# One table for all engines in the first chunk of a transformer block: x in two halves, weight groups between single products, three banks

## The reference

```
x = x + 0.5 * ffn(layernorm(x))
x = x + attention(layernorm(x))         # 16 heads of 16, causal
x = x + 0.5 * ffn(layernorm(x))
ffn:  W = LUT[4-bit codes] * scales     # gate, up: 2048 x 256; down: 256 x 2048; blocks of 32
      out = (gelu_tanh(x @ Wg.T) * (x @ Wu.T)) @ Wd.T
```

## Time and profile before

| what | us |
|---|---|
| median of 3 runs | 990.78 (986.47 to 992.03) |
| the profiled execution | 992.37 |
| its span, first to last instruction | 990.6 |
| TensorE busy | 926.6 |
| first product of the first chunk starts | 24.13 |
| first product of the second chunk starts | 107.91 |

### The profile page before, as it was taken

One profiled execution on the slowest core, in us unless ns is written; L12 is line 12 of the kernel. 1 busy time (PEld: TensorE's weight loads), 2 busy tenths in 40 slices (PEclk: granted clock), 3 DMA queues, 4 the chain that ended last, 5 costly groups with the idle time before them and its releaser, 6 DMA issues.

```text
span 990.6 us, 16766 instructions
## 1 busy us (share of the span) xinstructions
PE 926.6 (94%) x6726; PEld 408.9 (41%) x6726; DVE 611.1 (62%) x994; ACT 479.2 (48%) x650; POOL 230.5 (23%) x261
## 2 busy tenths in 40 slices
PE   2899999999989999888999989999999998999998
PEld 2456544554534545223544322244442222445444
DVE  6984345756777687677778767768785550242221
ACT  2454242033165330787332389963319999742240
POOL 3663573035002430000432000005200000052240
PEclk9999999999999999899999999999999999999999
DMA  7000050014000060000060000000000000000000
GB/s 262 1 1 1 1 96 11 2 57 52 2 2 2 25 83 2 1 1 2 1 107 2 22 2 2 1 1 1 2 22 2 1 2 2 2 1 1 22 1 21
DMA packets 19755, 20.26 MB, mean 20 GB/s; under 512 B 3040, under 2 KB 18400, under 8 KB 19680
## 3 DMA queue, kind: packets, MB, share of 16 engines
q1 hardware_dynamic: 16192, 15.93, 8.3%
q10 hardware_dynamic: 3488, 3.28, 1.0%
HBM read 12.78 MB, written 6.29 MB: 19 GB/s over the span
## 4 chain that ended last, share of the span: by engine, by line
PE 78%; ACT 6%; DVE 6%; issue 6%; DMA 2%; POOL 1%; SPq 0%; ACTq 0%; DVEq 0%; POOLq 0%
PE ps L1124 12%; PE ps L1095 12%; PE ps L1096 11%; PE ps L1097 11%; PE ps L1274 9%; PE ps L1229 7%; ACT inter L742 6%; PE ps L1125 6%; PE ps L1257 4%; DVE sg L1035 2%; DVE sg L1032 1%; PE ps L1241 1%; PE ps L1200 1%; PE ps L1080 1%; DMA xres<-in_L_attn_x 1%
## 5 line engine op out<-in xcount | busy, mean ns | idle before, releaser
L742 ACT ACTIVATE inter<-ps 128x1024 f32<-128x1024 f32 (+3 forms) x320 | 265.9, 898 | 34.9 <-PE ps L1241 19.3
L637 POOL TENSOR_TENSOR inter<-wreg,inter 128x512 f16<-128x512 f32 x112 | 129.3, 1158 | 644.6 <-ACT inter L723 644.4
L1035 DVE TENSOR_REDUCE sg<-ps 128x2 f32<-128x1024 f32 (+3 forms) x217 | 220.2, 1037 | 49.2 <-PE ps L1241 24.4
L752 ACT ACTIVATE wreg<-ps,gelu_in 128x512 f32<-128x512 f32 x112 | 77.1, 688 | 269.9 <-PE ps L1097 269.8
L1124 PE MATMUL ps<-wd,inter 128*128 128x512 f16 x512 | 170.8, 380 | 0.0
L1032 DVE TENSOR_REDUCE sg<-ps 128x1 f32<-128x512 f32 (+3 forms) x206 | 120.8, 632 | 64.7 <-PE ps L1229 43.7
L901 DVE SCALAR_TENSOR_TENSOR wreg<-ps,kappa,wreg 128x512 f32<-128x512 f32 x128 | 95.6, 748 | 102.8 <-PE ps L1097 97.0
L1274 PE MATMUL ps<-inter,v 128*17 128x512 f32 (+3 forms) x1280 | 150.1, 541 | 0.7
L1125 PE MATMUL ps<-wd,inter 128*128 128x256 f16 x512 | 139.5, 273 | 0.0
L1229 PE MATMUL ps<-kreg,qreg 48*128 48x512 f16 (+3 forms) x640 | 109.6, 355 | 18.4 <-DVE sg L1035 11.6
L1257 PE MATMUL ps<-qreg,kreg 50*128 50x512 f16 (+3 forms) x640 | 110.2, 354 | 16.2 <-ACT inter L742 10.6
(11 more groups left out here) (130 smaller groups left out, 890.6 us busy)
## 6 DMA issues: line engine op xcount, KB each, us to landing
qk_split<-oT SPq DMA_DIRECT2D x4, 1024.0 KB, 4.5
kreg<-qk_split SPq DMA_DIRECT2D x24, 128.0 KB, 4.7
qreg<-qk_split SPq DMA_DIRECT2D x24, 128.0 KB, 8.2
xres<-in_L_attn_x ACTq DMA_DIRECT2D x4, 512.0 KB, 5.5
out_x<-xres SPq DMA_DIRECT2D x4, 512.0 KB, 2.9
kreg<-in_L_ffn_gate_W_packed SPq DMA_DIRECT2D x4, 256.0 KB, 5.0
kreg<-in_L_ffn_up_W_packed ACTq DMA_DIRECT2D x4, 256.0 KB, 10.2
kreg<-in_L_ffn_down_W_packed SPq DMA_DIRECT2D x1, 1024.0 KB, 9.6
```

The source lines that it names most:

```text
L637: pool.tensor_tensor(inter[:, 1, u, :], prod_ring[:, u % 3, :], inter[:, 0, u, :], ALU.subtract).then_inc(s_inter, 1)
L742: act.activation(p_ring[:, pair % 8, :, 0:w], ps[:, 512 * b:512 * b + 1024].rearrange("p (a q) -> p a q", a=2)[:, :, 0:w], ACT.Exp, scale= ...
L1035: dve.tensor_reduce(m_part[:, r, part, col:col + 9:8], both[:, :, 0:width], AX.X, ALU.max).then_inc(s_slot_read, 1)
```

## The change

Nothing is computed otherwise; what changes is the order of the first chunk, and when transfers are asked for.

- x of the first chunk is loaded in two halves: tiles 0 and 1 by ScalarE's queue behind two loads of scales, tiles 2 and 3 by SyncE's behind scales and one piece of gate codes. The other chunks of x move from ScalarE's queue to the end of SyncE's.
- A single list, `first`, is followed by four engines. Products come as gate 0, gate 1, up 0, gate 2, up 1, gate 3 and so on, 32 with numbers 0 to 31. `DECODE_AT` says behind which product piece 2, 3, ... is decoded, `GROUP_AT` behind which product group 2, 3, ... is made, `OTHER_AT` places the statistics of the second chunk of x and the maxima of the attention's weights.
- Only groups 0 and 1 are transposed before the first product, and decode(1) stands behind the splitting of x. Groups go round three banks, 4, 5 and 6.
- x is transposed, copied and split by halves of two tiles, bank 6 and bank 7. The transposes of the second chunk's x move in between the second and the third token tile of the down products.
- ScalarE runs one gelu of a single column early. The little diagonal product of the maxima becomes a tensor_tensor.

The diff, without declarations and unchanged helpers:

```diff
@@ the table @@
-        W_BANKS = 2
-        FIRST_PIECES = 2
-        behind = [[] for _ in range(NT)]
-        for p, n in zip(range(FIRST_PIECES, 3 * NPIECE), (1, 2, 4, 5, 7, 8, 10, 11, 12, 13)):
-            behind[n] += [2 * p, 2 * p + 1]
-        behind[14] += [6 * NPIECE, 6 * NPIECE + 1]
-        behind[15] += [6 * NPIECE + 2, 6 * NPIECE + 3]
-        AMAX_TILE = 2
-        DECODE_AHEAD = 4
+        W_BANKS = 3
+        GROUP_AT = (0, 0, 1, 1, 3, 4, 6, 6, 11, 12, 13, 13, 16, 18, 18, 21, 22, 24, 26, 26, 28, 29, 29, 31, 31, 31)
+        DECODE_AT = (0, 0, 1, 3, 6, 10, 13, 14, 20, 23)
+        OTHER_AT = {10: ("statistics", 0), 12: ("statistics", 1), 14: ("statistics", 2), 16: ("statistics", 3),
+                    18: ("widest", 0), 19: ("normalise", 1), 20: ("widest rows", 2), 22: ("widest everywhere", 2),
+                    24: ("powers", 2)}
+        first = []
+        products = [("gate", 0), ("gate", 1)]
+        for n in range(NT):
+            products += [("up", n)] + ([("gate", n + 2)] if n + 2 < NT else [])
+        for i, product in enumerate(products):
+            first.append(product)
+            first += [("decode", 2 + p) for p, k in enumerate(DECODE_AT) if k == i]
+            first += [("weights", 2 + p) for p, k in enumerate(GROUP_AT) if k == i]
+            if i in OTHER_AT:
+                first.append(OTHER_AT[i])
@@ SyncE @@
             load_scales(sp, sg, gate_scales)
-            for q in range(NPIECE):
+            load_packed(sp, 0, 0)
+            load_x(sp, 0, slice(2, TPC), s_x_back)
+            for q in range(1, NPIECE):
                 load_packed(sp, 0, q)
...
+            for k in range(1, NCH):
+                load_x(sp, k, slice(0, TPC), s_x[k])
@@ GpSimd @@
-            for n in range(6):
-                decoded(n)
-                if n == 0:
-                    normalise(pool, own, 0, 0)
-            for n in range(NT):
-                pool.wait_ge(s_ihigh, n + 1)
-                pool.tensor_tensor(inter[:, 1, n, :], prod_ring[:, n % 3, :], inter[:, 0, n, :],
-                                   ALU.subtract).then_inc(s_inter, 1)
...
+            decoded(0)
+            normalise(pool, own, 0, 0)
+            decoded(1)
+            for kind, n in first:
+                if kind == "decode":
+                    decoded(n)
+                elif kind == "up":
+                    pool.wait_ge(s_ihigh, n + 1)
+                    pool.tensor_tensor(inter[:, 1, n, :], prod_ring[:, n % 3, :], inter[:, 0, n, :],
+                                       ALU.subtract).then_inc(s_inter, 1)
+                elif kind == "normalise":
+                    normalise(pool, own, n, JOBS[n][0])
@@ banks @@
-            return bank(k) if k in (2, 3) else bank(4 + k % W_BANKS)
+            return bank(4 + k % W_BANKS)
...
-        XT_BANKS = ps[:, 6 * 512:8 * 512].rearrange("p (k t) -> p k t", k=KT)
+        HALF = CT // 2
+        XT_BANKS = [bank(6 + h).rearrange("p (k t) -> p k t", k=KT) for h in range(2)]
@@ ScalarE @@
-            load_packed(act, 1, 0)
-            for k in range(NCH):
-                if k == 1:
-                    for q in range(1, NPIECE):
-                        load_packed(act, 1, q)
-                    act.wait_ge(s_packed[1][NPIECE - 1], 16)
...
+            load_x(act, 0, slice(0, 2), s_x[0])
+            for q in range(NPIECE):
+                load_packed(act, 1, q)
+            act.wait_ge(s_const, 1)
+            act.activation(gelu_ring[:, 2, 0:1], ident[:, 0:1], ACT.Gelu_apprx_tanh)
...
+                for kind, n in first:
+                    if kind == "gate":
+                        act.wait_ge(s_gate, n + 1)
+                        act.wait_ge(s_prod, 1 if n < 3 else n - 1)
+                        act.activation(gelu_ring[:, n % 3, :], bank(n % 2), ACT.Gelu_apprx_tanh,
+                                       scale=gelu_in[:, 0:1]).then_inc(s_gelu, 1)
+                        if n >= 2:
+                            high(0, n - 2)
+                    elif kind == "weights":
+                        weights_high(n)
+                high(0, NT - 2)
                 high(0, NT - 1)
-                x_high(1)
+                act.wait_ge(s_xt, 2)
+                x_high_half(0)
+                x_high_half(1)
...
             weights_high(0)
+            act.wait_ge(s_xt_first, 1)
+            x_high_half(0)
+            act.wait_ge(s_xt, 1)
+            x_high_half(1)
             weights_high(1)
-            x_high(0)
-            weights_high(2)
-            weights_high(3)
             first_chunk()
@@ VectorE @@
-                dve.tensor_scalar(amax_diag[0:count, 0:count], ident[0:count, 0:count], amax_top[0:count, 0:1], None,
-                                  ALU.mult).then_inc(s_amax_diag, 1)
+                dve.tensor_tensor(amax_diag[0:count, 0:count], ident[0:count, 0:count],
+                                  amax_top[0:count, 0:1].to_broadcast([count, count]), ALU.mult)\
+                   .then_inc(s_amax_diag, 1)
...
             aggregate()
-            decode(1)
             powers(1, slice(0, 3), W_POW + FP4_POW)
...
+            weights_low(0)
+            dve.wait_ge(s_xh_first, 1)
+            x_low_half(0)
+            dve.wait_ge(s_xh, 1)
+            x_low_half(1)
+            decode(1)
+            weights_low(1)
             own(dve.tensor_scalar(tmp1[:, :], pow_r[:, 0:1], pow_r[:, 1:2], 0.5 * 2.0 ** (-I_POW - W_POW),
                                   ALU.mult, ALU.mult))
...
-                for n in range(NT):
-                    product(0, n)
...
+                for kind, n in first:
+                    if kind == "up":
+                        product(0, n)
+                    elif kind == "decode":
+                        decode(n)
+                    elif kind == "weights":
+                        weights_low(n)
...
-            decode(2)
-            weights_low(0)
-            weights_low(1)
-            x_low(0)
-            weights_low(2)
-            decode(3)
-            weights_low(3)
-            decode(4)
-            decode(5)
@@ TensorE @@
-                if k >= 4:
+                if k >= W_BANKS:
                     pe.wait_ge(s_wl, k - W_BANKS + 1)
+                elif k == W_BANKS - 1:
+                    pe.wait_ge(s_xl, 1)
...
-                for n in range(NT):
-                    pe.wait_ge(s_wl, groups.index(("up", n // 2)) + 1 + (n == 1))
-                    gate(0, n)
-                    up(0, n)
-                    for k in behind[n]:
-                        transpose_weights(k)
...
-                transpose_x(1)
+                for kind, n in first:
+                    if kind == "gate":
+                        pe.wait_ge(s_wl, groups.index(("gate", n // 2)) + 1)
+                        gate(0, n)
+                    elif kind == "up":
+                        pe.wait_ge(s_wl, groups.index(("up", n // 2)) + 1)
+                        up(0, n)
+                    elif kind == "weights":
+                        transpose_weights(n)
...
                 pe.wait_ge(s_wl, 6 * NPIECE)
                 for m in range(TPC):
+                    if m == 2:
+                        pe.wait_ge(s_wl, len(groups))
+                        pe.wait_ge(s_yn, 2)
+                        for n in range(TPC):
+                            last = transpose_x(n)
+                        last.then_inc(s_xt, 1)
                     for part in range(4):
                         down(0, m, part)
```

More of the change, by code:

```diff
@@ L462, in load_scales, with load_x @@
                             src.rearrange("(q p r) b -> p q (r b)", p=P, r=TPC)).then_inc(s_scales, 16)
+        def load_x(queue, c, tiles, landed):
+            queue.dma_start(xres[:, TPC * D * c + D * tiles.start:TPC * D * c + D * tiles.stop]
+                            .rearrange("p (n d) -> p n d", d=D),
+                            x[0, CT * c + P * tiles.start:CT * c + P * tiles.stop, :]
+                            .rearrange("(n p) d -> p n d", p=P)).then_inc(landed, 16)
         ones_row = half_sum[0:3, 0, 0:P]
@@ L858, in _ @@
             for n in range(TPC):
+                if n == 2:
+                    dve.wait_ge(s_x_back, 16)
                 statistics(0, n)
@@ L915, in first_chunk @@
             def first_chunk():
-                for n in range(NT):
-                    product(0, n)
-                    if n == 4:
-                        dve.wait_ge(s_yn, 1)
-                    if 4 <= n < 4 + TPC:
-                        statistics(1, n - 4)
-                        step[0] += 1
-                    if n == 4 + TPC:
-                        dve.wait_ge(s_dve, step[0])
-                        aggregate()
-                    if behind[n] and behind[n][0] // 2 + DECODE_AHEAD < 3 * NPIECE:
-                        decode(behind[n][0] // 2 + DECODE_AHEAD)
-                    if n == AMAX_TILE:
+                for kind, n in first:
[5 more added lines that the diff above has]
+                        weights_low(n)
```

(35 more changed lines are left out.)

63 lines of the change are left out of this document (27 added, 36 removed).

## The result

| | before | after |
|---|---|---|
| median of 5 runs, us | 991.66 (986.47 to 992.39) | 984.11 (983.12 to 986.95) |
| ratio, 95% interval | | 0.9938, 0.9912 to 0.9965 |
| span of the profiled execution | 990.6 | 982.4 |
| first product of the first chunk | 24.13 | 15.65 |
| first product of the second chunk | 107.91 | 100.56 |

The change is 0.62% faster by the ratio of the runs, with an interval from 0.35 to 0.88%: about six microseconds, where 8.4 were forecast (between the two medians it is 7.55). The whole gain lies ahead of the second chunk, 7.35 us of the 8.2 by which the spans differ. The last line of the table is the same work in both kernels. For the experiments I read mainly where the second chunk starts.

The account below looks back on a forecast made before the run. TensorE, busy 94% of the span, was taken as the bound, so gains come from its waits, low clock or an earlier start. Head 7.7 plus stage 0.7 gave 8.4 us, 982.4 on the median; range 977.5 to 987.0.

Parts of the forecast that it names:

- The head: Stretch before the first chunk's first product: that product at 16.4 us instead of 24.13, 7.7 us earlier.
- x landed: Loading of the first chunk's x: landed between 5.7 and 8 us, anything up to 8.33 being equal.
- The diagonal product: VectorE step before the statistics: 1.03 us beside GpSimd's multiplication, ending at 8.33, so statistics begin 3.46 us earlier.
- Rival B: All TensorE waits but those for pieces 1 and 2 vanish, diagonal step short: gain 12.2 us, 978.6; chance 0.13.
- Statistics to normalising: Head, from statistics of x to its normalising: still 4.11 us, nothing saved, normalising starts at 12.44.
- Normalising: Four VectorE instructions in the head, 0.35 us apart without GpSimd's multiplications beside them: end 13.85, 1.6 us saved.
- Transposes and copies: Last part of the head, after normalising ends at 13.85: transposes end 14.9, copies and subtractions 16.4.
- The start of the products: Behind the first product: TensorE waits 0.9, 1.1 and 0.75 us, together 2.7, plus 0.5 us for low clock.
- The wait for the maxima: At product 20 TensorE waits for VectorE's reduction of the projections' maxima: 1.5 us, plus 1.0 for contention.
- Rival A: VectorE becomes the first chunk's bound, contention 4 us, later weight residues late: gain 4.4 us, 986.4; chance 0.27.
- Rival C: Pauses at the start keep TensorE's clock low; 5 us slower needs that until near 40 us; chance 0.04.
- rival D: The second chunk takes the gain back, waiting for DMA: same within 0.5%; chance 0.08 together with a weaker head.

Follow-up runs that it names:

- diagonal_behind_statistics: The changed kernel with the little diagonal product and the reduction ahead of it moved behind the statistics of x on VectorE; 986.01 us, ratio 0.9942.
- vector_load_early: The changed kernel with one unneeded VectorE instruction behind each of the first 8 products with up, ahead of the maxima reduction; 982.51 us, ratio 0.9909.
- maxima_read_early: The changed kernel with VectorE's reduction of the projections' maxima moved from behind product 18 to behind product 8; 980.37 us, ratio 0.9877.
- maxima_latest: The changed kernel with TensorE's maxima transposing behind product 24, spreading behind 26, powers behind 27, group 25 one product later; 985.59 us, ratio 0.9941.

## Why the prediction was right, and where not

**The head.** *x landed* between 5.7 and 8 us by forecast; 5.6 and 7.4. *The diagonal product* was put at 1.03 us; 1.02. Beside GpSimd's multiplication it takes the same time as a tensor_tensor as it did as a tensor_scalar; diagonal_behind_statistics gives its time behind both multiplications, 0.15. What the forecast calls a free port is VectorE with GpSimd idle beside it: the runs show these times, and no port. Rival B's 0.8 us for a short diagonal step was my estimate, and no run shows it: diagonal_behind_statistics, which moves the step, brought the first product 0.84 us forward, 0.23 of that from an earlier start, and the second chunk came 1.0 us later. *Statistics to normalising* was carried over as 4.11 us and measured 3.64, since GpSimd's three small steps and the hand-over were shorter by 0.47 (the first of them took 0.59 us before, beside a decode on VectorE, and 0.25 now). *Normalising* 1.4, measured 1.38. *Transposes and copies* 16.4 - 13.85 = 2.55, measured 2.5. In all 8.5 us earlier, with 7.7 forecast.

**The start of the products.** Forecast were waits of 0.9, 1.1 and 0.75 us, a low clock only for the first product and up(0) at 24.95 or 0.5 later. Measured were waits of 1.00, 0 and 0.30 us, the low clock up to gate(1), and up(0) at 24.63. VectorE's and GpSimd's chain for pieces 1 and 2 set it, as forecast; whether TensorE waits meanwhile or runs slowly was of no account, as up(0) 8.98 us behind the first product shows in kernels with one wait and with two. Against the first product the walk had 8.55 us, and 9.05 with the 0.5 for the clock. That the second comes close is luck: the 0.43 us missing in the walk are VectorE's, whose decode(3) took 3.15 us, and the clock cost nothing there.

**The wait for the maxima: the term that was mis-sized.** 2.5 us were given for it (1.5 walked, 1.0 added for contention). Counted from the first product, TensorE came there at 38.6 us, where the walk had 38.5, but the reduction ended at 41.9 instead of 40.0: VectorE's list was 1.9 us longer than walked, and not 1.0. The wait was 3.33 us, and the low clock behind it took another 1.2 us, which the sum did not have, though the earlier trace rows with its 1.94 us for a pair of groups showed just that price behind a wait of 3.55. So 4.6 instead of 2.5, and the stage from first product to second chunk was 84.9 us (before 83.8), 1.1 longer, where 0.7 shorter was forecast. The head was 0.75 better than forecast and the stage 1.8 worse: 7.35 us at the second chunk against 8.4. That the total came within the range with room is thus in part two misses of opposite sign.

**Rival A, VectorE as the bound,** was priced from its busy time, 52.3 us. This is where the reasoning failed without doing harm to the number: busy time was taken for work. vector_load_early added 2.6 us to a VectorE that was 95% busy from 34 to 44 us and 100% from 44 to 54, and nothing moved. The mean of 517 ns per step in the earlier trace rows contains standing time that shrinks when other work comes first: 532 ns in the changed kernel between 33 and 58 us, 414 with the load. How much more VectorE could have taken was not measured, nor how far GpSimd can be made to stand instead. The split of that room over the table stays open.

**Rival C, the clock,** needed a low clock from the first product until near 40 us. In the changed kernel it lasted, by the durations of the matmuls, from 15.65 to 22.4 us, where it cost nothing, and again from 57.7 to 60.5. But diagonal_behind_statistics showed it at work: a head 0.84 us faster, a chunk 1.0 us slower. The two low stretches shown in windows above, with 0.53 and 0.50, came behind a pause of 3.33 us and behind pauses of 2.27, 1.01 and 0.71 us. But the pauses alone do not tell: maxima_read_early paused for 1.00, 1.01 and 0.71 us at the same three places, and its up(0) ran at 0.38 us a matmul.

**Behind the first chunk** nothing was taken back (rival D): 881.8 us against 882.7.

## What to carry to other kernels

Move a load ahead of others by what its consumer can use: here the place in the queue gave 4 us, and a second queue nothing. When an engine looks fully busy, look for instructions of one form with two durations before calling it the bound. Here the long ones, 1.71 us for the two of a decode's second step where 0.75 also occurs, stood beside GpSimd's work, and 2.6 us of work placed in front of the reduction delayed nothing, with GpSimd standing instead (1.95 us where it had taken 1.41). Price a wait of TensorE together with the low clock behind it, here 1.2 us behind 3.33. And when a head gets faster, look at when the clock is low: the low stretch from 15.65 to 22.4 us was free, as TensorE would have waited there, and the one from 24 to 27.4 us in diagonal_behind_statistics cost 1.7 us, half its length.

## What the runs showed that I had not expected

The granted clock of a window reads 1.00 for the first microseconds of the changed kernel's products (15.60 to 19.00), while a 512-column matmul there took 0.61 to 0.64 us and later 0.38; there the durations are the better witness. When the clock rises differed between kernels whose heads are the same up to 0.3 us: the transposes for piece 1, the second work behind the first product, took 1.97 us in the changed kernel and 1.09 in maxima_read_early and maxima_latest. What decides that stayed open. And the same 882 us of work behind the first chunk took between 879.1 and 883.3 us in single executions, more than half of what the change is worth.
